# A GRU step on TensorE: two gates' low weights ahead of the low part's wait, and the first half's gates finished in the order r, n, z

## The reference

```python
def gru(x_seq, W_ih, W_hh, b_ih, b_hh):
    H = W_hh.shape[1]                       # 512
    pre_i = x_seq @ W_ih.T + b_ih           # all 1250 steps at once
    def step(h, pi):
        ph = h @ W_hh.T + b_hh              # W_hh is 1536 x 512
        r = jax.nn.sigmoid(pi[:H] + ph[:H])
        z = jax.nn.sigmoid(pi[H:2 * H] + ph[H:2 * H])
        n = jnp.tanh(pi[2 * H:] + r * ph[2 * H:])
        h_new = (1.0 - z) * n + z * h
        return (h_new, h_new)
    _, ys = jax.lax.scan(step, h0, pre_i)
    return ys
```

## Time and profile before

| what | us |
|---|---|
| median of 3 runs | 5277.53 (5269.09 to 5286.48) |
| the profiled execution | 5288.26 |
| its span, first to last instruction | 5286.2 |
| recurrence, first to last weight load of line 501 | 784.9 to 4148.7 |

### The profile page before, as it was taken

How to read it: one execution, slowest core, us unless ns; L and a number is a source line. 1 busy time by engine, 2 the same in 40 slices (tenths; PEclk the granted TensorE clock), 3 DMA queues, 4 the chain that set the end, 5 groups by cost and what they waited for, 6 DMA issues and landing times.

```text
span 5286.2 us, 338777 instructions
## 1 busy us (share of the span) xinstructions
PE 5071.3 (96%) x128234; PEld 4262.3 (81%) x128235; DVE 3006.4 (57%) x16450; ACT 2112.3 (40%) x15422; POOL 943.4 (18%) x5221
## 2 busy tenths in 40 slices
PE   5669999999999999999999999999999999999989
PEld 4555559999999999999999999999999645555654
DVE  6662336666666666666666666666666444355551
ACT  0110005555555555555555555555555201221110
POOL 1230002222222222222222222222222100000000
PEclk8559999999999999999999999999999998999989
DMA  1002220000000000000000000000000100001011
GB/s 59 0 3 97 80 87 0 0 0 0 0 0 0 0 0 0 0 0 0 0 0 0 0 0 0 0 0 0 0 0 0 54 8 10 35 35 35 19 46 45
DMA packets 28930, 81.07 MB, mean 15 GB/s; under 512 B 1594, under 2 KB 1834, under 8 KB 28858
## 3 DMA queue, kind: packets, MB, share of 16 engines
q1 hardware_dynamic: 28858, 80.03, 4.1%
HBM read 58.08 MB, written 21.95 MB: 15 GB/s over the span
## 4 chain that ended last, share of the span: by engine, by line
PE 92%; DVE 3%; issue 3%; DVEq 2%; ACT 0%; POOL 0%; DMA 0%; SPq 0%; POOLq 0%; ACTq 0%
PE psum L501 63%; PE psum L570 8%; PE psum L376 5%; PE psum L366 4%; PE psum L582 4%; PE psum L483 2%; PE psum L556 2%; PE psum L646 1%; PE psum L423 1%; DVE r L879 1%; DVEq L874 1%; DVE r L878 1%; DVEq L872 1%; DVEq L871 1%; PE psum L433 0%
## 5 line engine op out<-in xcount | busy, mean ns | idle before, releaser
L501 PE MATMUL psum<-h,r 128*128 128x16 f16 (+1 forms) x80000 | 3063.4, 181 | 11.1 <-ACT psum L706 4.4
L501 PEld LDWEIGHTS psum<-h,r 128*128 128x128 f16 x80000 | 2544.2, 96 | 113.0 <-ACT psum L706 5.0
L501 PE MATMUL psum<-h,hn 128*128 128x16 f16 (+1 forms) x40000 | 1801.3, 178 | 0.0
L501 PEld LDWEIGHTS psum<-h,hn 128*128 128x128 f16 x40000 | 1416.5, 96 | 0.0
L997 DVE TENSOR_TENSOR_SCAN psum<-mul_rz,psum 128x6 f32<-128x6 f32 x5000 | 871.6, 174 | 611.9 <-PE psum L501 563.1
L706 ACT COPY psum<-big 128x2 f32 (+1 forms) x7506 | 1002.8, 163 | 0.0
L328 POOL TENSOR_TENSOR upd_add<-upd,signs 128x4 f32<-128x4 f32 x2500 | 499.4, 200 | 2708.0 <-DVE h L1014 1524.0
L719 ACT ACTIVATE mul_n<-psum 128x2 f32<-128x2 f32 x2500 | 434.4, 174 | 1197.8 <-DVE psum L997 1197.8
L1011 DVE TENSOR_TENSOR_SCAN upd<-upd_mul,upd_add 128x8 f32<-128x8 f32 x2500 | 437.1, 175 | 414.1 <-ACT upd_mul L724 299.3
L728 ACT ACTIVATE upd_add<-psum 128x2 f32<-128x2 f32 x2500 | 433.4, 173 | 254.3 <-DVE psum L1003 238.7
L1003 DVE TENSOR_TENSOR_SCAN psum<-mul_n,psum 128x8 f32<-128x8 f32 x2500 | 446.8, 179 | 112.6
(11 more groups left out here) (231 smaller groups left out, 2791.2 us busy)
## 6 DMA issues: line engine op xcount, KB each, us to landing
ws<-in_Wl SPq DMA_DIRECT2D x9, 1024.0 KB, 5.3
ws<-in_Wr SPq DMA_DIRECT2D x9, 1024.0 KB, 7.7
edge_counts<-adj SPq DMA_DIRECT2D x2, 3051.8 KB
edge_weights<-big SPq DMA_DIRECT2D x1, 6103.5 KB
adj_rows<-big SPq DMA_DIRECT2D x1, 6103.5 KB
adj<-adj_rows SPq DMA_DIRECT2D x1, 6103.5 KB
big<-edge_counts SPq DMA_DIRECT2D x1, 6103.5 KB
adj<-edge_weights SPq DMA_DIRECT2D x1, 6103.5 KB
```

What stands on the lines that cost most here:

```text
L501: m = mm(places, whh16[g][:, part, 2 * kc + k, (2 * c + j) * P:(2 * c + j + 1) * P], state.unsqueeze(1).broadcast_to([P, COPIES, 2 - part] ...
```

## The change

It moves work on four queues and adds or removes none:

- TensorE, start of a step: the low-weight matmuls of z of half 0 (4) go in front of the wait for the low part, behind those of r. The high-weight ones of r and z then follow the wait.
- TensorE, n of half 1 from input half 0: the 4 matmuls (`every[:2]`) that stood in front of the wait for half 1's state join the other 4 behind r of half 1, together with their wait for `gru_put1`.
- TensorE, completion of half 0: n now goes ahead of z. ScalarE: `gate_z(0)` goes behind `gate_n(0)`. VectorE: `scan_n(t, 0)` goes ahead of z's scan.
- VectorE: the update of half 0 names its waits in the order z, n, as that of half 1 did already.

```diff
--- before.py
+++ after.py
@@ -508,23 +508,23 @@
                     t = 2 * i + u
                     pe.wait_ge(s("gru_state0"), 2 * t + 1)
                     pe.wait_ge(s("gru_put0"), t + 1)
-                    gru_gate(u, 0, 0, 0, part=1)
+                    for g in (0, 1):
+                        gru_gate(u, 0, 0, g, part=1)
                     pe.wait_ge(s("gru_state0"), 2 * t + 2)
-                    gru_gate(u, 0, 0, 0, part=0)
-                    for g in (1, 2):
-                        gru_gate(u, 0, 0, g)
+                    for g in (0, 1):
+                        gru_gate(u, 0, 0, g, part=0)
+                    gru_gate(u, 0, 0, 2)
                     pe.wait_ge(s("gru_put1"), 3 * t + 1)
                     gru_gate(u, 1, 0, 0)
-                    pe.wait_ge(s("gru_put1"), 3 * t + 2)
-                    gru_gate(u, 1, 0, 2, every[:2])
                     pe.wait_ge(s("gru_state1"), 2 * t + 1)
                     gru_gate(u, 0, 1, 0, part=1)
                     pe.wait_ge(s("gru_state1"), 2 * t + 2)
                     gru_gate(u, 0, 1, 0, part=0).then_inc(s("gru_r_mm0"), 1)
+                    gru_gate(u, 0, 1, 2).then_inc(s("gru_n_mm0"), 1)
                     gru_gate(u, 0, 1, 1).then_inc(s("gru_z_mm0"), 1)
-                    gru_gate(u, 0, 1, 2).then_inc(s("gru_n_mm0"), 1)
                     gru_gate(u, 1, 1, 0).then_inc(s("gru_r_mm1"), 1)
-                    gru_gate(u, 1, 0, 2, every[2:])
+                    pe.wait_ge(s("gru_put1"), 3 * t + 2)
+                    gru_gate(u, 1, 0, 2)
                     gru_gate(u, 1, 1, 2).then_inc(s("gru_n_mm1"), 1)
                     pe.wait_ge(s("gru_put1"), 3 * t + 3)
                     gru_gate(u, 1, 0, 1)
@@ -728,9 +728,9 @@
                         nc.scalar.activation(upd_add[:, c, 0:8:4], sum_n[c][:, 3:8:4], ACT.Tanh).then_inc(s(f"gru_n{c}"), 1)
 
                     gate_r(0)
-                    gate_z(0)
                     put(t + 1, 0, 0)
                     gate_n(0)
+                    gate_z(0)
                     gate_r(1)
                     put(t + 1, 0, 1)
                     put(t + 1, 0, 2).then_inc(s("gru_put0"), 1)
@@ -1004,7 +1004,7 @@
 
             def update(t, u, c):
 
-                for gate in "nz" if c == 0 else "zn":
+                for gate in "zn":
                     dve.wait_ge(s(f"gru_{gate}{c}"), t + 1)
                 dve.wait_ge(s(f"gru_kept{c}"), t + 1)
                 dve.wait_ge(s(f"gru_fresh{c}"), t + 1)
@@ -1023,8 +1023,8 @@
                 for u in range(2):
                     t = 2 * i + u
                     scan_rz(t, 0, 0)
+                    scan_n(t, 0)
                     scan_rz(t, 0, 1)
-                    scan_n(t, 0)
                     scan_rz(t, 1, 0)
                     update(t, u, 0)
                     high_part(u, 0)
```

## The result

The changed kernel takes 5325.65 us, median of 5 runs (5315.18 to 5328.77), against 5285.23 us before (5 runs, 5269.09 to 5293.69). The ratio is 1.0074, with a 95% interval from 1.0053 to 1.0095: slower, as forecast, by 40 us where 47 were worked out. The profiled execution has a span of 5326.7 us against 5286.2, and from the first to the last weight load of the recurrence it takes 3406.7 us against 3363.8, 43 more. So the loss lies in the recurrence.

The account below looks back on a forecast made before the run. Half 0's loop (2.69 us) was taken to bound the kernel; the change makes half 1's loop longest, (2.724 - 2.6864) x 1250 = 47 us more on a median of 5277.5, so 5324 us, range 5294 to 5348.

Parts of the forecast that it names:

- half 0's loop: First load through r of half 0, scan, update and high part: sets the pace at 2.69 us, 2.59 after the change.
- Part a: Low weights of z of half 0 ahead of the low part's wait: removes a 0.02 us stop.
- Part b: 4 loads of n of half 1 moved behind r of half 0: half 0's loop 0.105 us shorter, half 1's loop longer.
- half 1's loop: Low part's wait through the step's last load, scan of z, update, low part: 2.62 us before, 2.724 after, deciding.
- Part c: n ahead of z in half 0: update at 0.915 instead of 0.89 us, 0.02 worse in half 0's loop.
- The stops: TensorE's waits per step after the change: 0.06 at the seam, 0.04 and 0.10 at half 1's state, 0.20 us in all.
- third rival: TensorE's loop jump comes late and delays the 37th load in each second step: 5393 us, chance 0.03.
- first rival: Half 0's loop still decides, a step of 2.59 us, about 5150 us: chance 0.06.
- The second: TensorE's load rate sets the pace or terms cancel: 5265 to 5293 us, chance 0.09.

Follow-up runs that it names:

- low_alone: Kernel before with only the 4 low-weight matmuls of z of half 0 put ahead of the low part's wait: 5246.6 us, ratio 0.9937.
- block_alone: Kernel before with only the 4 matmuls of n of half 1 moved behind r of half 1: 5329.5 us, ratio 1.0097.
- block_back: Changed kernel with the 4 matmuls of n of half 1 back ahead of the wait for half 1's state: 5246.6 us replaced by 5246.2 us, ratio 0.9939.
- one_pair: Changed kernel with 2 of the 8 matmuls of n of half 1 ahead of the wait for half 1's state: 5272.0 us, one run.
- three_low: block_back plus half 0's high part before its float32 state, half 1's scan of n before half 0's low part, n's low weights before the wait: 5240.2 us, 0.9919.

## Why the prediction was right

- **The bound before.** That half 0's loop set the pace and half 1's had 0.06 us to spare was the centre of the argument. Both arms of the curve bear it out: 4 loads fewer ahead of the wait gave 2.720 (0.034 over before, not 0.105 under it), 4 more gave 2.763.
- **Part a**, 0.02 us off half 0's loop: low_alone has 2.661 in the mean against 2.686, 0.025.
- **Part b**, the decisive term: half 1's loop 2.724 worked out, 2.721 measured. The 3 ns are about the pitch (the distance from one load's start to the next): the 59 behind the 37th take 1.54 us, 26.1 ns each, where 26.3 with 0.005 off were taken. Over 1250 steps that is 4 of the 7 us between 47 and 40; the rest lies within the scatter of the medians. That 5324 and the measured 5325.7 agree to 2 us is luck in part: the forecast stands on the median of 5277.5 of three runs before, and the one beside the result is 5285.2.
- **Part c**, 0.02 worse in half 0's loop and hidden: the update starts 0.90 behind the scan of r where 0.915 was worked out and 0.89 stood before. The scan of z behind the scan of n is shorter than it is elsewhere (the pair at 2002.84 takes 0.30, and in the trace the first of it 0.160 instead of 0.174).
- **The stops.** Foreseen at the seam (0.06), at the 33rd load (0.04) and at the 37th (0.10). Where no jump comes before the step they are there, but otherwise divided: the run over the seam is 0.02 over its need, and the run of 16 0.17 where 0.14 were foreseen. The first load stands 1.28 behind the scan of r there, not 1.30, and what it gains is lost again at the 33rd (0.08). At a jump the seam alone takes 0.18 (1.02 - 0.84), and the run of 16 only 0.02. The time comes out the same, since the wait for half 1's low part ends when it ends.
- **The step that was mis-sized** is the third rival's: the next step was said to start 1.30 behind the scan of r, jump or not, and the 37th load to have 0.135 us to spare. At a jump the first load stood at 2003.77, 1.43 behind the scan of r at 2002.34, and of the margin 0.02 was left. Rows 3, with 1.00 and 0.99 at the two seams, gave no hint, because in those two the jump was hidden behind half 0's high part. One pair of seams was too little to read: in the trace of before 186 of the 372 steps with a jump between 2000 and 4000 us take 2.71 and the others 2.67 to 2.68, so half 0's loop is 2.68 and the mean of 2.686 has 0.008 of the jump in it, which the sum of 2.69, rounded to 0.01, could not tell apart. Moving 4 loads behind r of half 0 pushed the end of the step, and with it the jump, 0.1 later. Had it come 0.02 later still, every second step would have been longer.
- **The first rival** (2.59, about 5150 us) needed a half 1 loop under 2.69. With 0, 4 and 2 loads ahead, block_alone, block_back and one_pair put it at 2.72, under 2.66 and at 2.67. **The second**, TensorE's own rate: the loads were busy 387.4 of 400 us after and 387.6 before, the same number in a kernel with 0.20 us of stops in 2.72 and in one with 0.16 in 2.69; that share is blind to stops of this size.

## What to carry to other kernels

Where two dependent chains share one engine's queue, write both as loops (from the wait, through the loads queued behind it, to the instruction that ends the wait in the next round) and compare them with the engine's own work: a block moved from in front of a wait to behind it shortens one loop and lengthens the other by the same amount, so the best cut is where the two are equal, and the curve can be drawn before anything is run. Filler in front of a wait is not idle weight; it is what the other chain is hidden behind. And an instruction that comes earlier helps only until the next of the waits that start the same work (here ScalarE's copy, 0.02 earlier instead of 0.09), and only if nothing behind it in its queue comes later: look at what the swapped partner holds up.

## What was not expected of the hardware

- A loop body of 10 steps (1920 loads and matmuls) on TensorE is fetched again in each pass: 163 KB and 10 packets per pass on the instruction queue, a stop of 4.4 us in the rows shown, 1.24 times the time, and a mean granted clock of 0.886 instead of 0.963 over the run. The body of 2 steps is not (55 packets in all, as many as in the whole kernel before). Where between 2 and 10 steps the limit lies wasn't tried.
- The jump of the short loop takes TensorE 0.22 us from the last load of a pass to the first of the next (2003.55 to 2003.77) when nothing else hides it, against 0.03 between neighbours. In steps where the state comes at about the same time it has two lengths: from the last load to the first 0.17 or 0.22, so that in low_alone and three_low the step with a jump is 2.658 or 2.705. What chooses between them stays open.
- Three delays repeat to a few nanoseconds in all kernels, where nothing else holds the instruction: 0.25 to 0.26 from the last load of a gate to VectorE's scan, 0.05 from VectorE's end to the released load, 0.12 to 0.13 when the wait stands at a register instruction ahead of the load (the first wait of a step).
